# Two graph-attention layers behind one feature product: joined weights in the setup, and a new order of the loop body

## The reference, cut to what matters

```python
def _gat(h, adj, W, a, out_features):
    Wh = jnp.matmul(h, W)
    Wh1 = jnp.matmul(Wh, a[:out_features])
    Wh2 = jnp.matmul(Wh, a[out_features:])
    e = Wh1 + jnp.swapaxes(Wh2, 1, 2)
    e = jax.nn.leaky_relu(e, negative_slope=ALPHA)
    scores = jnp.where(adj > 0, e, NEG)
    att = jax.nn.softmax(scores, axis=1)
    return jnp.matmul(att, Wh)
...
h = _gat(x, adj, W1, a1, Fout)
h = _gat(h, adj, W2, a2, W2.shape[1])
h = _layernorm(residual + h, g_ln1, b_ln1)
residual2 = h
ff = jnp.matmul(jax.nn.relu(jnp.matmul(h, w_ff1) + b_ff1), w_ff2) + b_ff2
return _layernorm(residual2 + ff, g_ln2, b_ln2)
```

## Time and profile before

| | us |
|---|---|
| median of 3 runs | 3356.56 (3351.75 to 3358.59) |
| the profiled execution, its time | 3361.25 |
| its span, first to last instruction | 3359.4 |
| PE busy | 3151.1 |
| DVE busy | 2376.6 |
| ACT busy | 2228.8 |
| POOL busy | 1772.1 |

### The profile page before, as it was taken

One profiled execution on the slowest core, in us unless ns is written; L12 is line 12 of the kernel. 1 busy time (PEld: TensorE's weight loads), 2 busy tenths in 40 slices (PEclk: granted clock), 3 DMA queues, 4 the chain that ended last, 5 costly groups with the idle time before them and its releaser, 6 DMA issues.

```text
span 3359.4 us, 79402 instructions
## 1 busy us (share of the span) xinstructions
PE 3151.1 (94%) x27864; PEld 2840.8 (85%) x27864; DVE 2376.6 (71%) x5298; ACT 2228.8 (66%) x5770; POOL 1772.1 (53%) x1481
## 2 busy tenths in 40 slices
PE   4799999999999999999999999999999999999996
PEld 3688888888888888888888888888888888888885
DVE  4577776776776776776776776776776776776763
ACT  2466676676677677677677677677677676676673
POOL 1355555555555555555555555555555555555554
PEclk7899999999999999999999999999999999999998
DMA  5000000000000000000000000000000000000000
GB/s 127 20 27 29 22 28 28 22 28 28 22 28 28 23 27 28 25 25 28 26 25 28 27 24 27 28 25 25 28 25 25 28 25 25 28 25 25 28 10 14
DMA packets 98850, 93.43 MB, mean 28 GB/s; under 512 B 9856, under 2 KB 98048, under 8 KB 98816
## 3 DMA queue, kind: packets, MB, share of 16 engines
q1 hardware_dynamic: 98816, 92.97, 9.2%
HBM read 76.17 MB, written 16.78 MB: 28 GB/s over the span
## 4 chain that ended last, share of the span: by engine, by line
PE 86%; DVE 9%; issue 3%; ACT 1%; SPq 1%; POOL 0%; DMA 0%; DVEq 0%; POOLq 0%; ACTq 0%
PE ps_f L246 11%; PE ps_f L247 10%; PE ps_f L248 10%; PE ps_ao L436 7%; PE ps L426 7%; PE ps L246 4%; PE ps L248 4%; PE ps L247 4%; PE ps L416 4%; DVE s_least L819 4%; PE ps_ao L246 3%; PE ps_ao L247 3%; PE ps_ao L248 3%; PE ps_g L246 3%; PE ps_g L248 3%
## 5 line engine op out<-in xcount | busy, mean ns | idle before, releaser
L964 POOL TENSOR_TENSOR hid_lo<-hid_full,hid_hi 128x512 fp32r<-128x512 f32 x512 | 722.3, 1416 | 853.8 <-ACT hid_hi L601 847.0
L246 PE MATMUL ps_f<-down_w_hi,hid_hi 128*128 128x256 f32 x2048 | 602.1, 294 | 1.6 <-ACT hid_full L597 0.8
L247 PE MATMUL ps_f<-down_w_lo,hid_hi 128*128 128x256 f32 x2048 | 571.1, 279 | 0.0
L248 PE MATMUL ps_f<-down_w_hi,hid_lo 128*128 128x256 f32 x2048 | 570.7, 279 | 0.0
L616 ACT ACTIVATE prob<-ps,s_least 128x256 f32<-128x256 f32 x1024 | 471.3, 483 | 58.4 <-DVE s_least L819 57.5
L947 POOL TENSOR_TENSOR rstd<-vareps,neg_half 128x2 f32<-128x2 f32 x256 | 205.0, 801 | 442.0 <-DVE vareps L766 442.0
L246 PEld LDWEIGHTS ps_f<-down_w_hi,hid_hi 128*128 128x128 f32 x2048 | 384.4, 188 | 51.4 <-issue 45.3
L771 DVE TENSOR_SCALAR norm<-norm,meanvar,rstd 128x256 f32<-128x256 f32 x512 | 251.4, 533 | 198.4 <-POOL rstd L947 192.9
L247 PEld LDWEIGHTS ps_f<-down_w_lo,hid_hi 128*128 128x128 f32 x2048 | 386.9, 189 | 0.0
L828 DVE SCALAR_TENSOR_TENSOR masked<-adj_in,prob 128x1024 f32<-128x1024 int32 x256 | 386.9, 1550 | 0.0
L248 PEld LDWEIGHTS ps_f<-down_w_hi,hid_lo 128*128 128x128 f32 x2048 | 386.4, 189 | 0.0
(11 more groups left out here) (158 smaller groups left out, 9754.5 us busy)
## 6 DMA issues: line engine op xcount, KB each, us to landing
adj_in<-adj_keys SPq DMA_DIRECT2D x128, 256.0 KB, 2.8
xT_in<-x_features SPq DMA_DIRECT2D x64, 256.0 KB, 2.7
norm<-x_nodes SPq DMA_DIRECT2D x64, 256.0 KB, 2.7
out_nodes<-norm SPq DMA_DIRECT2D x64, 256.0 KB, 2.2
raw_up<-L_w_ff SPq DMA_DIRECT2D x1, 1024.0 KB, 5.5
raw_down<-L_w_ff SPq DMA_DIRECT2D x1, 1024.0 KB, 8.4
raw_v<-L_Wv SPq DMA_DIRECT2D x4, 256.0 KB, 7.6
raw_up<-L_W SPq DMA_DIRECT2D x1, 1024.0 KB, 9.2
```

What stands on the lines that cost most here:

```text
L246: nc.tensor.matmul(ps_out, left[0], right[0], start=first, stop=False)
L247: nc.tensor.matmul(ps_out, left[0], right[1], start=False, stop=False)
L248: return nc.tensor.matmul(ps_out, left[1], right[0], start=False, stop=last)
L964: pool.tensor_tensor(hid[1][:, 2 * m:2 * m + 2, :], hid_full[:, 2 * m:2 * m + 2, :], value(hid[0][:, 2 * m:2 * m + 2, :]), ALU.subtract).t ...
```

## The change

The weights of layer 1 are multiplied by those of layer 0 once, in the setup: since the first mix is linear, attention0 (x W0) W1 = attention0 (x (W0 W1)). The setup takes four transposes of W0 on PE, DVE's copy, four plain matmuls, another copy; the score vectors of layer 1 are then reduced against the joined weights. The features take one product of 260 columns: 256 of W0 W1, two scores of layer 1, two scores of layer 0. `pe_gat_mix` of layer 0 has attention as its left operand and 258 columns: it gives layer 1's features and scores at once, in natural layout, in the two banks of `ps_g`. Layer 1's own `pe_gat_rows` and `pe_gat_cols`, `act_h1`, `dve_h1` and their two events are gone.

All four body orders are rewritten. Every body gets one more flag, `nxt`, and a graph e = t + 3: `dve_fence`, `dve_gat_in`, `pool_gat_in` and `dve_gat_wh12(e, 0)` for the next graph stand late in the step before. A step -3 is added, in which PE has nothing. SP's order stays.

```diff
-        gat_w = [pair(f"gat_w{l}", [P, C, WE]) for l in range(2)]
+        gat_w = pair("gat_w", [P, C, WX])
-        def pe_gat_rows(pe, g, l):
-            if l == 0:
-                pe.wait_ge(*x_hi(g, 1))
-                pe.wait_ge(*x_lo(g, 1))
-                if not isinstance(g, int) or g > 0:
-                    pe.wait_ge(*hT_lo[0](g - 1, 1))
-            else:
-                pe.wait_ge(*h1_hi(g, 1))
-                pe.wait_ge(*h1_lo(g, 1))
+        def pe_gat_rows(pe, g):
+            pe.wait_ge(*x_hi(g, 1))
+            pe.wait_ge(*x_lo(g, 1))
+            if not isinstance(g, int) or g > 0:
+                pe.wait_ge(*ysum[0](g - 1, 1))
             for k in range(C):
-                last = product(ps_g[:, 0, 0:WE], cut(gT, k, nodes(0)), cut(gat_w[l], k), k == 0, k == C - 1)
-            last.then_inc(wh_done.sem, 1)
+                product(ps_g[:, 0, 0:WX], cut(gT, k, nodes(0)), cut(gat_w, k), k == 0,
+                        k == C - 1).then_inc(wh_done.sem, 1)
...
+        wh_cols = [slice(0, WE), slice(0, D)]
+        wh12_cols = [slice(D + 2, WX), slice(D, WE)]
         def pe_gat_mix(pe, g, l):
-            left, right = (wh, att_s) if l == 0 else (att_s, wh)
             for i in range(C):
+                mixed = ps_g[:, i, 0:WE] if l == 0 else ps_g[:, 0, i * D:(i + 1) * D]
                 for k in range(C):
-                    last = product(ps_g[:, 0, i * 256:(i + 1) * 256], cut(left, k, nodes(i)), cut(right, k),
-                                   k == 0, k == C - 1)
+                    last = product(mixed, cut(att_s, k, nodes(i)), cut(wh, k, wh_cols[l]), k == 0, k == C - 1)
...
+        def pe_gat_setup(pe):
+            pe.wait_ge(params_in[0], 16 * len(groups[0]))
+            pe.wait_ge(prep_p.sem, 4)
+            for i in range(C):
+                for f in range(C):
+                    last = nc.tensor.transpose(ps_f[:, 0, f * D + i * P:f * D + (i + 1) * P],
+                                               raw_gat[0][:, i, nodes(f)], ident[:])
+            last.then_inc(prep_t.sem, 1)
+            pe.wait_ge(prep_v.sem, W_TURNED)
+            for i in range(C):
+                for k in range(C):
+                    last = nc.tensor.matmul(ps_ao[:, 0, i * D:(i + 1) * D], raw_turned[:, k, nodes(i)],
+                                            raw_gat[1][:, k, :], start=(k == 0), stop=(k == C - 1))
+            last.then_inc(prep_t.sem, 1)
```

More of the change, by code:

```diff
@@ L97, in adj_seq_kernel @@
         raw_ctx = ExitStack()
-        raw_gat = [sb(f"raw_gat{l}", [P, C, WE], c=raw_ctx) for l in range(2)]
+        raw_gat = [sb(f"raw_gat{l}", [P, C, D], c=raw_ctx) for l in range(2)]
+        raw_turned = sb("raw_turned", [P, C, D], c=raw_ctx)
+        raw_both = sb("raw_both", [P, C, WX], c=raw_ctx)
         raw_a = [sb(f"raw_a{l}", [P, 2 * D], c=raw_ctx) for l in range(2)]
@@ L121, in adj_seq_kernel @@
         att_s, score = staged_pair("att_s", "score", [P, C, N])
-        wh = pair("wh", [P, C, D])
+        wh = pair("wh", [P, C, WE])
         wh12 = sb("wh12", [P, C, 2])
@@ L575, in act_gat_wh @@
             act.wait_ge(*wh1_done(g, l + 1))
-            act.activation(wh[0][:], ps_g[:, :, 0:D], ACT.Copy).then_inc(wh_hi.sem, 1)
+            act.activation(wh[0][:, :, wh_cols[l]], ps_g[:, :, wh_cols[l]], ACT.Copy).then_inc(wh_hi.sem, 1)
         def act_gat_exp(act, g, l):
@@ L659, in act_body @@
                 act_prob(act, b, 1, 0)
+            if gat:
+                act_gat_pre(act, c, 0)
+            if att1:
                 act_prob(act, b, 1, 1)
             if gat:
-                act_gat_pre(act, c, 1)
+                act_gat_wh(act, c, 0)
+                act_gat_exp(act, c, 0)
+                if isinstance(t, int) and t == -2:
+                    act_setup(act)
             if att1:
@@ L700, in dve_gat_wh12 @@
         def dve_gat_wh12(dve, g, l):
-            dve.wait_ge(*wh_done(g, 2 * l + 2))
-            dve.tensor_copy(wh12[:], ps_g[:, :, D:WE]).then_inc(wh12_set.sem, 1)
+            dve.wait_ge(*(wh_done(g, 2 * C) if l == 0 else mix_done(g, 1)))
+            dve.tensor_copy(wh12[:], ps_g[:, :, wh12_cols[l]]).then_inc(wh12_set.sem, 1)
         def dve_gat_wh(dve, g, l):
@@ L1009, in pool_body @@
                 pool_rstd(pool, d, 3)
+            if nxt:
+                pool_gat_in(pool, e)
+            if ff1:
                 pool_affine(pool, d, 3)
+            if att1:
+                pool_rstd(pool, b, 2)
+            if gat:
+                pool_hidden(pool, c, 0, 0)
+                pool_hidden(pool, c, 0, 1)
+                pool_hidden(pool, c, 0, 2)
+                pool_hidden(pool, c, 0, 3)
+            if ff0:
+                pool_rec_wide(pool, a, 0)
+                pool_affine(pool, a, 1)
+            if gat:
+                pool_rstd(pool, c, 1)
+            if ff0:
+                pool_rec_wide(pool, a, 1)
+            if att1:
+                pool_affine(pool, b, 2)
+                pool_hidden(pool, b, 1, 0)
+                pool_hidden(pool, b, 1, 1)
+                pool_hidden(pool, b, 1, 2)
+                pool_hidden(pool, b, 1, 3)
         def rows(w):
@@ L1025, in adj_seq_kernel @@
         groups = [
-            [(raw_gat[l][:, :, 0:D], rows(p0[f"W{l + 1}"])) for l in range(2)]
+            [(raw_gat[l][:], rows(p0[f"W{l + 1}"])) for l in range(2)]
             + [(raw_a[l][:], across(p0[f"a{l + 1}"].rearrange("n o -> (n o)"))) for l in range(2)],
@@ L1050, in adj_seq_kernel @@
         POOL_SPLITS = (1, 5)
-        gat_splits = [(raw_gat[l], gat_w[l]) for l in range(2)]
         TURNED_A = 2
-        WA = TURNED_A + 8
-        HI = WA + len(gat_splits)
-        LO = HI + len(gat_splits)
+        W_TURNED = TURNED_A + 2 * C + 1
+        W_BOTH = W_TURNED + 1
+        WA = W_BOTH + 2 * C
+        HI = WA + 1
+        LO = HI + 1
         GAT_READY = LO + 3 + R - 1
```

292 lines of the change are left out of this document (132 added, 160 removed).

## The result

| | before | after |
|---|---|---|
| median of the runs, us | 3355.08 (4 runs, 3351.75 to 3358.59) | 3297.48 (4 runs, 3295.86 to 3299.18) |
| span of the profiled execution, us | 3359.4 | 3297.4 |

The ratio is 0.9828, 95% interval 0.9811 to 0.9845: 1.7% faster. That is 58 us where 181 were forecast, and outside the range of 3125 to 3262.

A forecast was written before the change was run, and what follows sets the result against it. PE's queue was taken as the bound, at 50.30 us a body. Per body -1.43 - 1.78 + 0.5 = -2.7 us, over sixty bodies -162, with -13 and -6 at the ends -181: 3176 us, range 3125 to 3262.

The forecast's parts named there:

- The removed product: Layer 1's feature product, 12 matmuls of 258 columns, leaves PE's queue: net -1.43 us a body.
- Rival 1: PE's waits come back elsewhere, so only the product's 1.43 us a body is gained: 3252 us, chance 0.19.
- The two waits of now: PE's waits for POOL's gT_lo (1.31 us) and DVE's score-column copy (0.47) both go: -1.78 us a body.
- The new order, laid out: PE's groups set end to end, 47.1 us a body, with the other engines' queues beside them to find new waits.
- New waits: PE waits 0.35 us before reach and 0.15 before av(b,0) in the new order: +0.5 us a body.
- PE's own pace: Twelve 256-column products take 1.36 or 1.44 us; the mix may shift by +0.4 to -0.8 us a body, 0 taken.
- Start: New setup is covered by the bias loads, PE's old setup begins earlier, at about 46 us: -13 us in all.
- end: Last body gains its product and wait, but the last norm is 1.3 us later: -6 us in all.
- Rival 3: Slower: DVE's chain before reach, stretched by POOL, holds PE up; 3416 us with 4 us more a body, chance 0.05.
- the prediction's own signs of a miss: Forecast is wrong if PE's waits exceed 1.2 us a body or its busy time falls by other than 1.4.

The follow-up runs named there:

- e5: The kernel before with only the joined weights and single product of 260 columns, bodies in the old order: 3357.52 us, ratio 1.0005 to before.
- e4: The changed kernel with its feature product made twice into the same banks (12 more split matmuls): 3347.43 us, body 50.24 us.
- e2: The changed kernel with light POOL passes (low halves copied, gain and shift left out): 3154.74 us, body 47.18 us.
- e11: The changed kernel with one constant fill in place of each POOL low-half, gain and shift pass: body 47.05 us.
- e1: The changed kernel with POOL's low half of the next graph's features moved ahead of rstd(d,3): 3238.75 us, body 48.55 us.
- e3: The kernel before, in its old order, with light POOL passes (low halves copied, gain and shift left out): 3406.13 us.
- e8: The changed kernel with the moves of e1, e6 and e7 together: 3398.99 us, ratio 1.0124 to before.
- e6: The changed kernel with norm(b,2) ahead of norm_end(d,3) in DVE's queue: 3431.42 us, body 51.61 us.
- e7: The changed kernel with PE's reach, v(b,0) and flag one product later each, turn(a,1) behind the last mix: 3332.21 us.

## Why the prediction was wrong, by its steps

The forecast body was 47.6 us and the measured one 49.52: 60 times 1.9 is 115 of the 119 us by which the span missed.

- **The removed product, -1.43:** right as work, 1658.30 to 1659.74 for the one that is left. As a gain it stood only in the sum with free waits; by itself it was worth 0.0 in the old order (e5) and half in the new (e4). Rival 1's "only the product goes" was too good as well. The formula that the prediction quotes from the Trainium skill, "TensorE: Matmul & The Clock Gate", section "Back-to-back issue gap", is by that page the gap of an isolated matmul. The figure that the page has for a stream with weight loads, about 131 ns at 512 columns, isn't borne out: v's matmuls of 512 columns start 0.23 us apart (1664.34, 1664.57, 1664.80 after).
- **The two waits of now, -1.78:** gT_lo's 1.31 went. wh's 0.47 became 0.33: the cover of 1.8 us that PE got was used up by DVE, which reached wh12 only when the masks had ended at 1661.88.
- **The new order, laid out:** the groups of PE were right, 47.18 (e2) and 47.05 (e11) for 47.1. **The step that failed is the DVE chain laid beside them.** Its lengths came from rows where POOL was idle (norm_end 0.75), and only the masks were taken stretched. Measured: norm_end(b,2) 1.96, and 3.44 for the masks, for which 3.66 was taken. The two other norm_ends, 0.74 alone, took 1.68 and 1.74; the first held up up(a,0,1), which the prediction didn't name, the second turn(a,1). DVE was put at 36.1 us a body and had 42.49.
- **New waits, +0.5:** this term was mis-sized: 1.60, and about 0.2 us of refilling (more busy time of PE) at each wait, which the sum left out: four, 0.87 (49.52 - 47.05 - 1.60), and in e1 three, 0.56 (48.55 - 47.05 - 0.94). The place "before reach" was right, 0.21 for 0.35 (the prediction's own terms add up to 12.47 against 12.2, which is 0.3); before rec_wide there was none.
- **PE's own pace, 0:** its bad end came. q's twelve products, 1.36 in the earlier trace rows, take 1.42 with the joined weights (1687.87 to 1689.29 after), also in e5, which has the old order, and 1.36 in e3, which has the old weights. With some seven groups of twelve at the fast pace before, it costs an estimated 0.4 us a body, hidden in the 47.1, where the missing refilling made up for it. What sets the pace stays open.
- **Start -13, end -6:** -8.25 and -7.8, 16 for 19. PE's setup began at 44.84, for 46 forecast.
- **Rivals:** rival 1 (waits come back elsewhere) is what happened, with 0.19; its time of 3252 left out that longer DVE rows bring waits of their own. Rival 3's mechanism, stretching beside POOL, was the cause, though far below its price. Both of the prediction's own signs of a miss are in the profile: waits over 1.2 us a body, and PE's busy time down by 0.62 (48.52 to 47.90) where 1.4 were forecast.

A look at the earlier trace rows would have done: the same pair of masks at 2.42 and 3.66, with POOL's passes at 3.52 for two beside it. The prediction applied that to the masks and to nothing else.

## What to carry to other kernels

Before a new order is laid out, read each DVE and POOL row at its shortest and at its longest, see what the other engine ran at that time, and lay the new order out with the lengths that its own overlaps give. A removed piece of work is worth what the queue behind it can use: ask what is late next. Where two engines hold each other up, move the pass that disturbs (e1: one instruction, 0.97 us a body), and test one move at a time: each of the three in e8 had its reason, two of them cost 4.1% and 1.1% of the changed kernel by themselves (e6, e7), and together they cost 3.1%.

## What the runs showed of the hardware

TensorE's granted clock fell after some waits of 2.07 us (e3) and of 2.32 us (e6), in the middle of a body in which it was otherwise busy. Windows of e6 (the last three columns are clock, DMA share, GB/s):

```profile
1722.00:1724.00 2.00, 0.03 (x1) 0.00 (x0) 2.00 (x2) 1.07 (x6) 1.14 (x1) 1.00 0.22 77
1724.00:1725.00 1.00, 0.65 (x3) 0.32 (x4) 1.00 (x4) 0.00 (x0) 0.00 (x0) 0.59 0.00 0
1725.00:1726.00 1.00, 1.00 (x7) 0.96 (x7) 1.00 (x2) 0.84 (x2) 0.00 (x0) 0.50 0.00 0
```

A clock of 0.50 is the lower of the two levels. The twelve matmuls behind the wait took 2.62 us (1725.11 to 1727.73). One body earlier PE had waited as long at the same place, and the clock stayed:

```profile
1673.74 0.43 PE L285 MATMUL ps_g<-ident,wh 128*128 128x128 f32 x2 [2.32 <-DVE wh L697]
```

```profile
1674.00:1675.00 1.00, 0.79 (x8) 0.61 (x7) 1.00 (x2) 0.79 (x2) 0.00 (x0) 1.00 0.00 0
1675.00:1676.00 1.00, 1.00 (x12) 1.00 (x11) 1.00 (x6) 0.60 (x4) 0.12 (x1) 1.00 0.00 0
```

There the same twelve took 1.49 us (1674.50 to 1675.99). A fall costs 1.3 us of a body (51.92 against 50.61). It came after 34 of 60 such waits in e3 (2.07 us), 40 of 59 in e6 (2.32) and 12 of 60 in e8 (2.25), so the length of the wait by itself doesn't decide it; what does stays open. After the waits of 1.12 (e5) and 1.31 (before) shown above the clock stayed at 1.00.
